# Low parts of query weights on VectorE, each block in its neighbour's memory; sums of squares between the query and key products

## What is computed

```python
def _L0_cond_ref(x, emb, W_emb, b_emb, g_norm, W_qkv, g_q, g_k, W_out):   # 16 heads of 32
    scale, shift = jnp.split(emb @ W_emb + b_emb, 2, axis=-1)
    xn = _rms_norm(x, g_norm) * (1.0 + scale) + shift
    q, k, v = heads(xn @ W_qkv)                 # W_qkv: 512 x 1536
    q = _rms_norm(q, g_q)                       # over the 32 numbers of a head
    k = _rms_norm(k, g_k)
    attn = jax.nn.softmax(q @ k.T * d ** (-0.5), axis=-1)
    o = attn @ v
    return o + o @ W_out

def _L0_ffn_ref(x1, ...):                       # 4-bit weights with a scale for each 64
    x2 = relu(x1 @ w_up + b_up + x1 @ w_up_lora_a @ w_up_lora_b)
    return x2 @ w_down + b_down + x2 @ w_down_lora_a @ w_down_lora_b

x = x + _L0_ffn_ref(_L0_cond_ref(x, cond_2048[:, None, :], ...), ...)
x = x + _L1_ffn_ref(_L1_cond_ref(cond_2048, cond_2048, x, ...), ...)
```

## Time and profile before

| | us |
|---|---|
| median of 3 runs | 2893.96 |
| lowest, highest | 2891.05, 2894.92 |
| the profiled execution | 2898.88 |
| its span, first to last instruction | 2897.1 |
| layer 0, batches 0 to 7 | to about 870 |
| mean granted clock of PE | 0.965 |

### The profile page before, as it was taken

The page is one execution under the profiler, slowest core; times in us unless marked ns, Lnnn a source line. Parts: engine busy times, 40 slices in busy tenths (PEclk is TensorE's granted clock), DMA queues, the critical chain, the costliest instruction groups (busy, mean ns, idle before and its releaser), DMA issues.

```text
span 2897.1 us, 132208 instructions
## 1 busy us (share of the span) xinstructions
PE 2714.9 (94%) x49688; PEld 2397.8 (83%) x49696; DVE 1806.4 (62%) x6366; ACT 1139.6 (39%) x4994; POOL 1364.0 (47%) x3476
## 2 busy tenths in 40 slices
PE   7487988888899999999999999999999999999998
PEld 5265766676687778999999999999999999999987
DVE  4665675565565556666666666666666666666654
ACT  3343345456544333334334333333433433433322
POOL 2422001112116665665666666666666666666600
PEclk8699999999999998999999999999999999999999
DMA  7622344344420003444444444444444444444376
GB/s 218 203 70 70 95 131 144 114 154 159 140 91 3 4 28 98 129 131 131 132 127 135 128 130 129 136 127 127 136 127 129 134 132 128 130 134 130 117 236 201
DMA packets 138459, 363.74 MB, mean 126 GB/s; under 512 B 15968, under 2 KB 25312, under 8 KB 137696
## 3 DMA queue, kind: packets, MB, share of 16 engines
q1 hardware_dynamic: 137568, 357.06, 40.1%
q10 hardware_dynamic: 672, 3.67, 0.3%
HBM read 324.62 MB, written 34.47 MB: 124 GB/s over the span
## 4 chain that ended last, share of the span: by engine, by line
PE 60%; POOL 5%; issue 3%; DVE 2%; DMA 0%; ACT 0%; POOLq 0%; DVEq 0%; SPq 0%
PE pscan L1504 12%; PE pd L1457 12%; PE pg L1409 12%; PE pscan L1500 12%; PE pu L1409 11%; POOL lin L1254 1%; POOL lin L1270 0%; POOL from_q L1266 0%; POOL carry L1299 0%; POOL lin L1264 0%; POOL lin L1276 0%; POOL from_q L1272 0%; POOL from_q L1281 0%; POOL lin L1285 0%; PE prouter L1519 0%
## 5 line engine op out<-in xcount | busy, mean ns | idle before, releaser
L1500 PEld LDWEIGHTS pscan<-th,carry 128*128 128x128 f16 x16384 | 551.1, 96 | 71.7 <-ACT th L1319 50.4
L1500 PE MATMUL pscan<-th,carry 128*128 128x8 f16 x16384 | 560.3, 166 | 19.5 <-ACT th L1319 8.7
L1504 PE MATMUL pscan<-th,carry 128*128 128x16 f16 x16384 | 558.2, 169 | 1.6 <-DVE th L1615 1.1
L1504 PEld LDWEIGHTS pscan<-th,carry 128*128 128x128 f16 x16384 | 482.3, 96 | 2.8 <-DVE th L1615 2.1
L1319 ACT ACTIVATE th<-state 128x32 f16<-128x32 f32 x768 | 175.9, 229 | 688.5 <-DVE state L1632 688.5
L1457 PE MATMUL pd<-hg,wbuf 128*128 128x256 f16 x3168 | 429.3, 274 | 2.6 <-DMA wbuf<-w_split 2.6
L1409 PE MATMUL pg<-qh,wbuf 128*128 128x256 f16 x3168 | 427.3, 274 | 0.0
L1409 PE MATMUL pu<-qh,wbuf 128*128 128x256 f16 x3168 | 423.1, 272 | 0.0
L1632 DVE TENSOR_REDUCE state<-pscan 128x32 f32<-128x96 f32 x768 | 197.7, 257 | 263.2 <-PE pscan L1504 257.4
L1409 PEld LDWEIGHTS pg<-qh,wbuf 128*128 128x128 f16 x3168 | 295.0, 98 | 36.6 <-issue 0.3
L1409 PEld LDWEIGHTS pu<-qh,wbuf 128*128 128x128 f16 x3168 | 292.4, 97 | 31.9
(11 more groups left out here) (273 smaller groups left out, 4774.7 us busy)
## 6 DMA issues: line engine op xcount, KB each, us to landing
wbuf<-w_split SPq DMA_DIRECT2D x264, 512.0 KB, 3.5
wbuf<-w_split SPq DMA_DIRECT2D x264, 384.0 KB, 3.1
parts_mem<-in_w_tiles SPq DMA_DIRECT2D x149, 256.0 KB, 3.2
w_split<-parts_mem SPq DMA_DIRECT2D x99, 256.0 KB, 2.8
late<-in_w_tiles SPq DMA_DIRECT2D x49, 256.0 KB, 3.5
w_split<-spare SPq DMA_DIRECT2D x33, 128.0 KB, 3.1
out<-oo SPq DMA_DIRECT2D x8, 512.0 KB, 3.6
w_qkv<-in_w_qkv ACTq DMA_DIRECT2D x1, 3072.0 KB, 10.0
```

What stands on the lines that cost most here:

```text
L1500: mm(pscan[:, 0, m * B:(m + 1) * B], clo[:, k, m * P:(m + 1) * P], th[:, k, 0, :], start=(m == 0 and k == 0), stop=False, skip_group_check ...
L1504: ins = mm(pscan[:, 0:2, m * B:(m + 1) * B], chi[:, k, m * P:(m + 1) * P], th[:, k], start=False, stop=(k == NC - 1), skip_group_check=True)
```

## The change

It has six parts.
1. *Low halves on VectorE.* GpSimd's two instructions for each block go. VectorE makes the low half in one (`weights_low`), at the end of each round of batch 1, behind that round's last low halves. ScalarE's high half of block c is written beside it into the memory of block c-1, which is free by then; block 0 goes to `home`, in `parts_mem`, and one DMA brings it to the memory of block 3. ScalarE's conversions of blocks 1 to 3 stand behind `widened(c-1)` of their round. `wqkv(k, ...)` finds block k in its new place.
2. `widest_qkv` and GpSimd's reduction move from the head of batch 1 to the end of batch 0.
3. *Sums of squares.* `head_norm(c-1)` stands between query and key product of block c, not behind both. ScalarE's order stays.
4. `split_parts` deals two tiles instead of three to each slot of the head stage, and so one more to each of four heads' slots.
5. In VectorE's order, the low half of the fourth of a round's places stands ahead of the fourth copy, not behind it.
6. The second addition of a feed-forward layer (`second(n, 1)`) stands at its last place instead of the next one's first.

```diff
+        home = parts_mem[:, 3 * N:6 * N]
+        home16 = home.bitcast(F16).rearrange("p (h n) -> p h n", h=2)
+        def split_home(c):
+            return home16 if c == 0 else w16[:, c - 1]
+        def wqkv(k, half, cols):
+            return w16[:, (k + NC - 1) % NC, half, cols]
...
         def split_parts(b, at):
-            return spread((b - 4) * 25, 25, at, 3, PARTS) if b >= 4 else []
+            return spread((b - 4) * 25, 25, at, 2, PARTS) if b >= 4 else []
...
                 if n == 16 + DEPTH:
-                    for c in range(NC):
-                        sp.wait_ge(S["w_lo"], c + 1)
-                        sp.dma_start(w16[:, c, 1, :], high_home[c % 2]).then_inc(S["w_back1" if c % 2 else "w_back0"], 16)
+                    sp.wait_ge(S["w_lo"], NC)
+                    sp.dma_start(w_qkv[:, NC - 1, :], home).then_inc(S["w_back"], 16)
...
-                if b == 1:
+                if b == 0:
                     pl.wait_ge(S["w_max"], 1)
                     pl.partition_all_reduce(tops[:, 0:17], tops[:, 0:17], P, bass.bass_isa.ReduceOp.max).then_inc(S["w_all"], 1)
-                    pl.wait_ge(S["w_scale"], 1)
-                    pl.wait_ge(S["p_qk"], SPLIT * NC)
-                    for c in range(NC):
-                        pl.wait_ge(S["w_hi"], c + 1)
-                        pl.tensor_scalar(w_qkv[:, c, :], w_qkv[:, c, :], for_w, None, ALU.mult).then_inc(S["w_scaled"], 1)
-                        pl.wait_ge(S["w_scaled"], c + 1)
-                        pl.tensor_tensor(w16[:, c, 0, :], w_qkv[:, c, :], high_home[c % 2], ALU.subtract).then_inc(S["w_lo"], 1)
...
-                        if c >= 2:
-                            act.wait_ge(S["w_back1" if c % 2 else "w_back0"], 16)
-                        act.activation(high_home[c % 2], w_qkv[:, c, :], ACT.Identity, scale=for_w).then_inc(S["w_hi"], 1)
+                        else:
+                            act.wait_ge(S["w_lo"], c)
+                        act.activation(split_home(c)[:, 1, :], w_qkv[:, c, :], ACT.Identity, scale=for_w).then_inc(S["w_hi"], 1)
                 weights_wide(0)
-                weights_wide(1)
...
                     if c:
                         widened(c - 1)
+                        weights_wide(c)
...
-                    if c >= 2:
-                        weights_wide(c)
...
+                        if c and a == 0:
+                            head_norm(c - 1)
                     ins.then_inc(S["p_qk"], 1)
-                    if c:
-                        head_norm(c - 1)
...
+            def weights_low(b, c):
+                if b == SPLIT - 1:
+                    if c == 0:
+                        dve.wait_ge(S["p_qk"], SPLIT * NC)
+                    dve.wait_ge(S["w_hi"], c + 1)
+                    dve.scalar_tensor_tensor(split_home(c)[:, 0, :], w_qkv[:, c, :], for_w, split_home(c)[:, 1, :], ALU.mult, ALU.subtract).then_inc(S["w_lo"], 1)
...
-                if b == SPLIT - 1:
-                    widest_qkv()
...
                     inverse(c)
+                    lows(b, ffn_quad[c][3:4])
                     turned(h + 3)
-                    lows(b, ffn_quad[c][3:])
+                    lows(b, ffn_quad[c][4:])
+                    weights_low(b, c)
                     if c == 2 and b + 1 < B:
                         normed_input(b + 1)
                 gathered(NC - 1)
+                if b == 0:
+                    widest_qkv()
...
                 for n, part in ffn_work(b, places):
-                    if part == 0 and n:
-                        second(n - 1, 1)
                     if part < HC and part % 2:
                         hidden_low(n, part // 2)
                     if part == WORK - 4:
                         second(n, 0)
+                    if part == WORK - 1:
+                        second(n, 1)
```

More of the change, by code:

```diff
@@ L147, in layer0 @@
         part_in = [parts_mem[:, a * N:(a + 1) * N] for a in range(3)] + [late[:, 2 * NC * T:2 * NC * T + N]]
-        high_home = [parts_mem[:, 1536 + 768 * i:1536 + 768 * (i + 1)].bitcast(F16) for i in range(2)]
+        home = parts_mem[:, 3 * N:6 * N]
[4 more added lines that the diff above has]
+            return w16[:, (k + NC - 1) % NC, half, cols]
         part_out = [parts_mem[:, (3 + a) * N:(4 + a) * N].bitcast(F16).rearrange("p (h n) -> p h n", h=2) for a in range(3)]
@@ L169, in layer0 @@
                  "mm_lora scaled stage split d_bounds g_bounds lora_scale lora_high lora_ok "
-                 "w_max w_all w_scale w_hi w_scaled w_lo w_back0 w_back1 "
+                 "w_max w_all w_scale w_hi w_lo w_back "
                  "part_in0 part_in1 part_in2 part_in3 part_out0 part_out1 part_out2 part_hi part_done part_third third_out widest gmax wscale state_in mx par coef setup").split()
@@ L631, in batch @@
                 if split:
-                    pe.wait_ge(S["w_back0"], 16 * NC // 2)
-                    pe.wait_ge(S["w_back1"], 16 * NC // 2)
+                    pe.wait_ge(S["w_back"], 16)
                 def values(after):
@@ L638, in values @@
                                 for x_, w_ in ((0, 1), (0, 0), (1, 1)):
-                                    ins = mm(Ob[i][:], xn16[:, k, x_, i * P:(i + 1) * P], w16[:, k, w_, 2 * N:3 * N],
+                                    ins = mm(Ob[i][:], xn16[:, k, x_, i * P:(i + 1) * P], wqkv(k, w_, slice(2 * N, 3 * N)),
                                              start=(k == 0 and w_ > x_), stop=(k == NC - 1 and x_ == 1))
@@ L660, in batch @@
                                 for w_, x_ in ((1, 0), (1, 1), (0, 0)):
-                                    ins = mm(gbank(b, c)[:, a * T:(a + 1) * T], w16[:, k, w_, cols], xn16[:, k, x_, :],
+                                    ins = mm(gbank(b, c)[:, a * T:(a + 1) * T], wqkv(k, w_, cols), xn16[:, k, x_, :],
                                              start=(k == 0 and w_ > x_), stop=(k == NC - 1 and w_ == 0))
@@ L1001, in batch @@
                 dve.tensor_reduce(span, x1, AX.XY, ALU.max, apply_absolute_value=True).then_inc(S["d_span"], 1)
-                if b == B - 1:
-                    second(B - 3, 1)
                 if b == B - 1:
```

## The result

The changed kernel takes 2908.03 us (median of 7 runs, 2905.34 to 2911.49) against 2894.92 us of the kernel before in 7 runs (2891.05 to 2904.07): 13.1 us more, ratio 1.0039, 95% interval 1.0024 to 1.0053. Forecast was 6.1 us more, with 2886 to 2908 as the range, so the time stands on its upper bound, 0.03 us past the 2908 as written. The direction was right, the size about half of what came. The profiled execution is 2909.70 us, its span 2907.9, against 2898.88 and 2897.1.

What follows compares the result with a forecast made beforehand. PE, busy 94% of the span, was taken as the bound, so time moves only with its waits or clock. Terms -2.8 + 2.5 + 4.5 - 0.1 + 2 = +6.1 us gave 2900.0 us at the median, range 2886 to 2908.

Steps and rivals of the forecast that it cites:

- the head stages: Batches 2 to 7, each from its first product to its first transposition: +2.5 us over all six.
- the rounds: Batches 2 to 7, groups of four heads from the first transposition on, and output products between them: +4.4 us.
- Weight parts: Batch 1: stall and DMA wait go, but most of the gain is spent in the first three rounds; -2.8 us.
- Maximum moved: Head of batches 0 and 1: moving the 6.54 us maximum over the query weights gains nothing; zero.
- Sums between the products: Head stage: logarithm +0.72 us later per link, third product +0.7, fourth +1.4; +2.5 us together with fewer tile parts.
- Tiles: Batches 4 to 7, fewer tile parts before row maxima: with the moved sums -1.0, +0.9, -0.7 and +0.6 us.
- Low parts: Ahead of a round's fourth copy, batches 2 to 7: they delay the next scores or sums; +4.5 us.
- Clock: PE behind longer head-stage gaps: more stretches at the lower level; +2 us, between -2 and +7.
- the stall goes and the added work hides: Rival: batch 1 gains 8.0 + 1.5 us, 2 to 3 lost at the head stage; -7, 2887 us; chance 0.19.
- waits take the losses up: Rival: waits before the next transposition absorb head-stage and low-part delays; about 0, 2894 us; chance 0.27.
- The clock as the main cause: Rival: the lower level follows the longer gap in each of six batches, twice; up to 7 us, 2907; chance 0.10.
- The stall staying: Rival: batch 1's stall has another cause and remains; 6.2 us on top of the 6.1, 2906; chance 0.03.

Runs made afterwards that it cites:

- weights alone: The kernel before with only the weight parts and their maximum moved: 2895.50 us, ratio 0.9991 to the kernel before.
- sums undone: The changed kernel with the sums of squares back behind both products, all else as changed: 2891.25 us, ratio 0.9985 to the kernel before.
- sums alone: The kernel before with only the sums of squares moved between query and key product: 2911.97 us, ratio 1.0046 to the kernel before.

## Why the prediction was right or wrong, step by step

The direction and two mechanisms were right. That the time came out on the edge of the range and not beyond it is in part luck: the head stages were put 4.6 us too high, and the rounds 6.2 too low, or 4.2 if the clock's 2 belong there.

- **Weight parts**, -2.8 us: right, -2.6 measured alone. So was its form: the instruction is 1.81 us for 1.8, the scalings 0.41, PE's gap 3.29 in a forecast of 3 to 4. In the changed kernel itself batch 1 gained nothing, since its first scores started 2.4 us later than before, mostly by batch 0's output products at 9.47 us for 7.14, and its head stage lost 0.8.
- **Maximum moved**, zero: not contradicted. It ends 153.5 us in, beside the output products, and the addition behind it starts at once. With the weights alone, the maximum over the output sum starts 7.9 us behind the first output product, as before.
- **Sums between the products**: the mechanism was right to its rows (logarithm directly behind the square), the links were a little large (0.58 us each, for 0.72 and 0.86). The term that was mis-sized is what they cost in all: +2.5 for sums and tiles in one. The sums cost 13.3 us alone and 15.6 in the changed kernel, of which the longer waits are 6.9. In the changed kernel the rest is mostly the first scores' wait and the clock, as placed under sums undone.
- **Tiles**: they hid that loss. The prediction had batches 4 to 7 at -0.2 with sums and tiles, for +1.2 and +1.5 in batches 2 and 3 with the sums only, so about 6 us in all for the smaller share, and nothing to the four parts that go to the heads' slots ("there PE's own 1.9 us per head cover them"). The runs show 13 to 14 us saved in the head stages and 5 to 8 lost in the rounds. This is why the head stages came out at -2.1 for +2.5 (tiles -13.3, sums +14.3), and it is half of why the rounds came out at +10.6 (tiles +5.5, low parts +5.3).
- **Low parts**, +4.5: mis-sized, 6.9, 7.8 and 12.4 in three pairs of kernels. The scores' part is 3.3 us. What was left out is the last round, where no scores follow but the weighted values of that round wait for the same copy: "the other places" listed only scores and sums. That is 2 to 3.4 us, and the clock behind it in batches 5 and 6.
- **Clock**, +2: the reason was weak, the size at that place was not. I took batch 2 for one case and batch 4 for the other and did not count the batches between: five of six of the kernel before already ran below 0.70 there. Between the two profiles the six stretches cost 1.1 us more (7.6 for 6.5); over ten kernels, five at each wait, the mean is 2.4 more, near the 2. What it missed is the clock in the last rounds of batches 5 and 6 and ahead of batch 1.
- **Rivals.** That the stall goes and the added work hides is refuted by the weights alone. That waits take the losses up is refuted by sums alone. The clock as the main cause is refuted as it was put: the lower level came behind the first wait in five of six batches before and after, and behind the second in none. The stall staying is refuted by 1.06 us for three scalings.
- **Sum.** By kernels that differ by one step each: weights alone -2.6, with tiles and second additions -8.7 more (to 0.9961), with the low parts +6.9 (to 0.9985), with the sums +15.6 (to 1.0039), together 11.3 before rounding. Measured apart, the sums are 13.3 and the tiles beside moved sums 4, so how much belongs to which part depends on what else is there, by a few us that the intervals do not settle.

The page "SBUF — State Buffer" of the Trainium skill, section "SBUF: two separate sides", held where the trace could show it: the stall of 7.55 us went with GpSimd's instructions, and the new weight instructions, with none of GpSimd's beside them, took 1.807 to 1.810 us. Whether they would wait for such an instruction was not tried.

## What to carry to other kernels

When work is moved earlier on one engine, read its consumer's queue first: an earlier result is worth nothing if the consumer has an instruction ahead of it that waits for something later, and here the same move was +13 us with the old order behind it and -27 with one swap. When an instruction is put ahead of another, list everybody who waits for the second one, in the last round of the loop too. And before a pattern is taken from two rows, count it over all repetitions.

## What was not expected of the hardware

Behind the third product's wait of 1.04 us PE was granted 1.00 in all 24 cases of four kernels. A wait of 2.35 us was followed by less than 0.70 in 15 of 30, one of 2.93 us in 22 of 30, and a wait of 1.62 us, ahead of the fourth product, in none of 30. So taking 1.3 us off a wait gave back up to 1.5 us more. The same output products, 32 of 128x256, took from 7.14 us at a granted clock of 1.00 to 9.86 at 0.72.
